# The recurrent state steps placed after the first FFN, with the second norm and the transposed Gram blocks spread over three steps

## What is computed

```python
def step(c, xt):
    ft = sigmoid(xt @ wf.T + c @ uf.T + bf)
    it = sigmoid(xt @ wi.T + c @ ui.T + bi)
    gt = tanh(xt @ wc.T + c @ uc.T + bc)
    return ft * c + it * gt
h = tanh(x @ wo.T + c_final @ uo.T + bo)
```

```python
S = S * lam
err = v_t - einsum('bhk,bhkv->bhv', k_t, S)
S = S + beta * k_t[..., :, None] * err[..., None, :]
o_t = einsum('bhk,bhkv->bhv', q_t, S)
```

## Time and profile before

| | us |
|---|---|
| median of 3 runs | 1555.78 |
| the profiled execution | 1562.62 |
| its span | 1560.8 |
| TensorE busy in it (matmul) | 1380.0 (88%) |
| VectorE busy | 924.6 (59%) |
| ScalarE busy | 689.2 (44%) |
| GpSimd busy | 197.3 (13%) |
| TensorE in the chain that ended last | 61% |
| VectorE in that chain | 21% |
| "issue" in that chain | 9% |

### The profile page before, as it was taken

One profiled execution on the slowest core, in us unless ns is written; L12 is line 12 of the kernel. 1 busy time (PEld: TensorE's weight loads), 2 busy tenths in 40 slices (PEclk: granted clock), 3 DMA queues, 4 the chain that ended last, 5 costly groups with the idle time before them and its releaser, 6 DMA issues.

```text
span 1560.8 us, 61982 instructions
## 1 busy us (share of the span) xinstructions
PE 1380.0 (88%) x27811; PEld 1277.7 (82%) x27811; DVE 924.6 (59%) x2208; ACT 689.2 (44%) x1585; POOL 197.3 (13%) x230
## 2 busy tenths in 40 slices
PE   4889899998989899888888988889899999999887
PEld 4878798888979788777877887878788989898776
DVE  2646686777867766558655774664444645554532
ACT  2253454545445444443444444344445445444332
POOL 0001010010100100002400320040130404040400
PEclk9999999998999989998889979989999999999999
DMA  4011112112211323232224222421534333332000
GB/s 128 1 41 68 42 44 84 58 75 67 78 63 58 124 64 95 91 119 65 73 82 131 68 90 64 158 70 47 166 88 119 98 110 107 90 122 80 28 28 28
DMA packets 64201, 125.39 MB, mean 80 GB/s; under 512 B 12352, under 2 KB 33088, under 8 KB 61888
## 3 DMA queue, kind: packets, MB, share of 16 engines
q1 hardware_dynamic: 63936, 121.43, 24.3%
HBM read 62.13 MB, written 59.24 MB: 78 GB/s over the span
## 4 chain that ended last, share of the span: by engine, by line
PE 61%; DVE 21%; issue 9%; ACT 7%; DVEq 0%; ACTq 0%
PE ps L426 29%; PE ps L493 7%; PE ps L1007 6%; PE ps L818 4%; PE ps L642 4%; PE ps L991 4%; DVE ln_bn L83 3%; ACT gates L443 3%; PE ps L667 2%; ACT ffn_rows L101 2%; DVE ig L469 2%; PE ps L386 1%; ACT gates L450 1%; PE ps L478 1%; DVE prod L743 1%
## 5 line engine op out<-in xcount | busy, mean ns | idle before, releaser
L426 PE MATMUL ps<-cst,wt 128*128 128x128 f32 x2688 | 360.7, 290 | 8.3 <-DVE cst L471 7.8
L426 PEld LDWEIGHTS ps<-cst,wt 128*128 128x128 f32 x2688 | 331.3, 201 | 20.0 <-DVE cst L471 9.1
L426 PE MATMUL ps<-ffn_rows,wt 128*128 128x128 f32 x2304 | 300.3, 288 | 17.4 <-DVE hs L506 6.4
L426 PEld LDWEIGHTS ps<-ffn_rows,wt 128*128 128x128 f32 x2304 | 285.7, 203 | 25.9 <-issue 15.8
L465 DVE TENSOR_TENSOR fc<-gates,cst 128x256 f32<-128x256 f32 x112 | 51.7, 461 | 285.0 <-ACT gates L443 284.9
L443 ACT ACTIVATE gates<-ps,colv 128x128 f32<-128x128 f32 x448 | 127.1, 365 | 173.9 <-PE ps L426 173.6
L1007 PE MATMUL ps<-e,kgb 32*128 32x64 f32 x4032 | 129.6, 275 | 7.9 <-issue 4.1
L1007 PEld LDWEIGHTS ps<-e,kgb 32*128 32x128 f32 x4032 | 120.6, 189 | 16.6 <-issue 10.6
L1096 POOL TENSOR_TENSOR ffn_rows<-ffn_rows,rowv 128x256 f32<-128x256 f32 x64 | 54.3, 882 | 573.5 <-DMA ffn_rows<-x_scratch 573.5
L818 PE MATMUL ps<-inv_cols,kv 32*32 32x32 f32 x8192 | 92.4, 201 | 34.3 <-DVE zbd L1037 17.4
L618 POOL TENSOR_TENSOR kg_rows<-key_rows,g_tok 128x512 f32<-128x512 f32 x32 | 46.4, 1478 | 594.9 <-DVE key_rows L581 594.9
(11 more groups left out here) (117 smaller groups left out, 1793.5 us busy)
## 6 DMA issues: line engine op xcount, KB each, us to landing
kg_scratch<-kg_rows SPq DMA_DIRECT2D x32, 512.0 KB, 3.9
xs_scratch<-xs_out SPq DMA_DIRECT2D x32, 512.0 KB, 3.6
xsb<-xs_scratch SPq DMA_DIRECT2D x64, 256.0 KB, 3.5
kgb<-kg_scratch SPq DMA_DIRECT2D x256, 64.0 KB, 2.6
ffn_rows<-x SPq DMA_DIRECT2D x32, 256.0 KB, 3.4
x_scratch<-ffn_rows SPq DMA_DIRECT2D x32, 256.0 KB, 2.7
e_scratch<-e SPq DMA_DIRECT2D x256, 32.0 KB, 1.7
ffn_rows<-e_scratch SPq DMA_DIRECT2D x8, 1024.0 KB, 6.2
```

Of the source, the lines that this page charges most:

```text
L426: mm = pe.matmul(banks[g][:, col:col + P], wt[:, w, k, m * P:(m + 1) * P], rhs, start=(x in (0, FI)), stop=(k == KT - 1 and (t == 0 or x > ...
```

## The change

SOLO becomes 8, so all of the first FFN runs in solo blocks, and SECOND becomes JOIN + 16 = 80. Hops 0 to 14 run in steps 65 to 79, in which no FFN runs; hops 15 to 63 still run beside the second FFN, now in steps 80 to 128. In steps 64 to 79 the part 0 pieces stand between a hop's two products, the part 1 pieces behind its update. The load of x1 into the buffer of a block moves from t = 1 to t = 2 (blocks whose successor by two does not exist). The program ends at step 146 instead of 130.

`PERIOD` is rearranged: gt0 moves ahead of the norm's statistics in t = 0; the norm is cut into statistics (`ln2`, t = 0) and coefficients (`lc2`, t = 1), its application into two halves (`apa`, t = 1, and `apb`, t = 2); lt1, v01, v23 and tt0, tt1, ta0, ta1, ta2 each move half a step to a step later; the first norm's pieces (`ln1`, `lc1`, `ap0`, `ap1`) move half a step earlier. The three steps over which norm and transposed Gram blocks spread are t = 0, 1 and 2.

```diff
-          1: ([(3, "ta4"), (2, "gt0")], [(2, "gt1"), (3, "ta5"), (2, "inv1"), (1, "apply")]),
+          1: ([(3, "ta4")], [(2, "gt1"), (1, "lc2"), (3, "ta5"), (1, "apa")]),
...
-SOLO = 6
+SOLO = NB
...
-SECOND = TILE * NB
+SECOND = JOIN + 2 * TILE
...
                 ln2.stats_bn(dve, n, xt[b.p], bn_buf[0])
+            elif name == "lc2":
                 ln2.coefficients_bn(dve, n, bn_buf[0])
...
-                ln2.apply(act, n, xn2, xt[b.p], range(8))
+                ln2.apply(act, n, xn2, xt[b.p], range(4) if name == "apa" else range(4, 8))
...
+                act.wait_ge(ln2.applied, 8 * (n + 1))
                 act.activation(key_half, key_rows, ACT.Square).then_inc(sq_done, 1)
...
+            if t == 2 and prep.real and not prep.ahead(2).real:
+                sp.wait_ge(ln2.applied, 8 * (prep.n + 1))
+                sp.wait_ge(x_out[prep.p], prep.quarters_landed)
+                sp.dma_start(xt[prep.p], x1_d[prep.n + 2 - NB]).then_inc(x1_in[prep.p], 16)
...
                 if s is not None:
                     hop_states_pe(pe, s)
...
+                if b is None:
+                    pieces(pe, *period_of(i, 0), prep_pe, solve_pe)
+                else:
+                    fg.pe_step(pe, b, t, *((0, NX) if t == 0 else (NX, NX + FI)))
...
                 if s is not None:
                     hop_update_pe(pe, s)
...
+                if b is not None:
+                    if t > 0:
+                        fg.pe_step(pe, b, t, NX + FI, 2 * NX)
...
                 pieces(pe, *period_of(i, 1), prep_pe, solve_pe)
```

More of the change, by code:

```diff
@@ L222, in fill_table @@
         b, t = divmod(i, TILE)
-        n = b - NB
-        if t == 0 and n < NB:
-            singles((4, 5) if i == JOIN else (2,), *four(*(("fr1", b) if n < 0 else ("fr2", n)), (2, 3)))
+        n = b - SECOND // TILE
+        if t == 0 and 0 <= n < NB:
+            singles((2,), *four("fr2", n, (2, 3)))
+        if n < 0:
+            for behind, name in PERIOD[t][0]:
+                piece(name, b - behind)
         if hop_at(i) is not None:
@@ L228, in fill_table @@
             ahead_of_hop[last_hop] = list(counts)
-        for behind, name in PERIOD[t][0] + PERIOD[t][1] + (LAST_GRAM if t == TILE - 1 else []):
+        if n >= 0:
+            for behind, name in PERIOD[t][0]:
+                piece(name, b - behind)
+        for behind, name in PERIOD[t][1]:
             piece(name, b - behind)
         if t == TILE - 1:
-            if n + 1 < NB:
-                singles((4, 5), *four(*(("fr1", b + 1) if n + 1 < 0 else ("fr2", n + 1)), (0, 1)))
+            for behind, name in LAST_GRAM:
+                piece(name, b - behind)
+            if 0 <= n + 1 < NB:
+                singles((4, 5), *four("fr2", n + 1, (0, 1)))
             for behind, name in LAST_UNIT:
                 piece(name, b - behind)
-            if n < NB:
-                singles((2,), ("ct1", b) if n < 0 else ("ct2", n))
+            if 0 <= n < NB:
+                singles((2,), ("ct2", n))
     return table, behind_hop, ahead_of_hop
@@ L1129, in second_pe @@
             for i in range(JOIN, END):
-                f, b, t = step_of(i)
+                b, t = step_of(i)
                 s = hop_at(i)
-                old, done = ending(i)
-                new, nxt = starting(i)
+                done, nxt = ending(i), starting(i)
                 if s is not None:
                     hop_states_pe(pe, s)
-                for r in range(2):
-                    if done is not None:
-                        old.pe_h(pe, done, 2 + r)
-                    if t == 0 and f is not None and r == 0:
-                        f.pe_front(pe, b, (2,))
@@ L1175, in second_act @@
                 post_act(act, i, 0)
-                if t == 0 and f is not None:
-                    if i == SECOND:
-                        act.wait_ge(ff.h_full, 4 * NB)
-                    f.act_front(act, b, (2,))
-                if f is not None:
-                    f.act_step(act, b, t, (0,))
+                if b is None:
+                    pieces(act, *period_of(i, 0), prep_act, solve_act)
+                else:
                     if t == 0:
-                        f.act_front(act, b, (3,))
+                        fg.act_front(act, b, (2,))
+                    fg.act_step(act, b, t, (0,))
+                    if t == 0:
+                        fg.act_front(act, b, (3,))
                 if s is not None:
                     state_act(act, s)
-                if f is not None:
-                    f.act_step(act, b, t, (1,))
+                if b is not None:
+                    fg.act_step(act, b, t, (1,))
                 if i == JOIN:
                     for j in (2, 3):
-                        ff.act_h(act, Block(SOLO - 1), j)
+                        ff.act_h(act, Block(NB - 1), j)
                 if done is not None:
-                    for j in (2, 3) if old is ff else range(4):
-                        old.act_h(act, done, j)
-                for part in range(2):
-                    pieces(act, *period_of(i, part), prep_act, solve_act)
+                    for j in range(4):
+                        fg.act_h(act, done, j)
+                if b is not None:
+                    pieces(act, *period_of(i, 0), prep_act, solve_act)
+                pieces(act, *period_of(i, 1), prep_act, solve_act)
                 post_act(act, i, 1)
@@ L1198, in second_act @@
                     pieces(act, Block(i // TILE), LAST_GRAM, prep_act, solve_act)
[L1199 to L1205 removed]
+                    if nxt is not None:
+                        if nxt.n == 0:
+                            act.wait_ge(ff.h_full, 4 * NB)
+                        if nxt.n == 1:
+                            act.wait_ge(kg_out, 64 * NB)
+                        fg.act_front(act, nxt, (0, 1))
                     pieces(act, Block(i // TILE), LAST_UNIT, prep_act, solve_act)
[L1207 to L1209 removed]
         def second_dve(dve):
             for i in range(JOIN, END):
[L1213 removed]
+                b, t = step_of(i)
                 s = hop_at(i)
[L1215 removed]
+                done = ending(i)
                 if i == SECOND + TILE:
```

122 lines of the change are left out of this document (54 added, 68 removed), and 12 rows, old and new, of the table PERIOD.

## The result

The changed kernel takes 1651.12 us (median of 4 runs, 1650.19 to 1653.08) against 1559.35 for the kernel before in the same measurement (1555.32 to 1564.24): a ratio of 1.0589, 95% interval 1.0548 to 1.0629. The forecast was 1575, with a range of 1530 to 1614. The direction was right, the size was not: +92 us where +19 was forecast. The profiled execution took 1651.69 us against 1562.62, so the two traces differ by 89.1, and all of it can be placed.

The account below looks back on a forecast made before the run. TensorE, busy 87 to 96% of every kind of block, was taken as the bound. 190 + 213.5 + 90 + 410 + 6 = 909.5, less 890.9, gave +19: 1581 profiled, a median near 1575, range 1530 to 1614.

Parts of the forecast that it names:

- H: Stretch from FFN block 7's last cell state through steps 64 to 79, without FFN: 213.5 us, ends 190 and 235.
- +1 a block: Solo blocks 2 to 7: new waits of 7.4 nearly cancel 7.7 gone; +1 us each taken, +6 in sum.
- lt1 waits for lt0's copies, 1.7 and 0.4: Solo blocks: new waits of 1.7 and 0.4 us, as ScalarE copies lt0 after the second apply and the gates.
- The stall goes, and with it what followed at half clock: 7.7: Solo blocks: the 3.65 us stall before gt1 and the half-clock work behind it vanish, 7.7 us.
- Ends -4 and +5 a block: Solo blocks 2 to 7: range around the forecast change of +1 us each.
- Rival 3: Clock stays down in H (232 us) and after the ta0 wait (+5 a solo block): +61, 1617 us; chance 0.12.
- The hand-drawn chain: H: state-step ring added up from update to update for steps 65 to 80, 195.5 us before hand-overs and clock.
- 12 for the clock: H: 12 us added for a quarter of some 100 us of TensorE work running half-rate.
- The 6 for hand-overs: H: 6 us added for hand-overs between engines, four a step at 0.1.
- The supply term (5): H, step 72: 5 us for instruction supply, about one and a half waits of 3.39; ends 0 and 10.
- Rival 1: Solo blocks: old bank wait goes with its half clock, 7.7 each in six, new waits hidden: 1523 us; chance 0.20.
- rival 2: State ring is short, H = 195, solo blocks as before: -6, 1550 us; chance 0.18.

Follow-up runs that it names:

- Run 7: The changed kernel with the transpose of alpha moved behind v01, from t = 2 to t = 3: 1625.18 us, ratio 1.0411.
- Run 9: The kernel before, its placement kept, with a separate table in solo blocks (parts of the change, alpha behind v01): 1548.56 us, ratio 0.9940.
- runs 4 to 6: The changed kernel with added matmuls nobody reads in steps 65 to 79, of 128, 512 and 384 columns: 1650.22, 1649.17 and 1654.18 us.
- run 1: The changed kernel's placement of the state steps with the table of the kernel before: 1603.09 us, ratio 1.0258.
- run 10: The changed kernel, all eight blocks solo and its table in H, with the solo table of Run 9 in solo blocks: 1580.84 us, ratio 1.0102.
- run 3: The kernel before with only the norm's coefficients moved behind the read of gt1: 1578.84 us, ratio 1.0107.

## Why the prediction was wrong

**Right.** What runs where; that H is a ring of state steps with waits on other engines in every round; its waits at the places named (the inverse ahead of a unit read, 9.80; pieces for the state copies, mostly 1.6); the clock under 0.85 (it was 0.60); block 0 (86.6 for 90) and blocks 1 to 5 (411.4 for 410); the wait ahead of ta0 (4.09 for 3.8) and ahead of gt0 (1.49 for 1.5); that the ta0 wait is followed by the half clock. Of the other signs, TensorE was to be about half busy in H (it was for 68%, since the same work took longer), and the solo blocks were to take 94 to 98 (98 to 106 for blocks 2 to 7).

**Wrong, the solo blocks: the step "+1 a block".** Forecast +6, measured +49. It failed in three of its parts.
- "lt1 waits for lt0's copies, 1.7 and 0.4". The copies are late as described, but the piece that meets them first is the transpose of alpha, which shares a bank and stands ahead of the x part. Lt1 comes behind that x part and finds them done. The wait is 3.88, with nothing to fill it. Run 7 takes it away: -26 us, the clock's part included. In the order on TensorE the alpha row stands between lt0 and the x part; I priced lt1 and not this row.
- "The stall goes, and with it what followed at half clock: 7.7". The stall went, the half clock did not: it followed the new waits (4.16 and 4.29), and the one of 1.49 ahead of gt0 as well (its transposes took 1.94 for 1.0). Busy time rose, by 0.7 in block 5, 5.3 in block 6 and 2.1 in block 7, each against the old block 5. The +1 was all that I left for the clock, when the row of 3.65 and 5.31 had shown what a wait of that length brings. Run 9 sizes the gain at 3.1 where smaller waits of 2.6 stand in the stall's place. (The x part's full-clock row is the 2.92 of the earlier trace rows, not the 2.84 of the cell-state part; 0.1 of the 7.7.)
- "Ends -4 and +5 a block" was too narrow: with two unpriced items of the same sign the true value was about +8.

Rival 3 had the clock's return behind the ta0 wait, but +5 a block; it lacked alpha's 3.88.

**Wrong by size, H.** Forecast 213.5, measured 243.0, beyond the end of 235. The hand-drawn chain held in its kind: no step was shorter than drawn, the long ones (65, 69, 72, 75) by 0.5 to 2.0 longer, the short ones (70, 71, 73, 74, 78) by 4 to 6. The term that was mis-sized is "12 for the clock", twice over. I let a quarter of TensorE's work run half-rate; the granted clock says about 80% of the time did (a mean of 0.60 between levels of 0.5 and 1). And I priced half rate by the unit product (1.93 for 1.29, a half more), while the update, the largest group in the ring, took 3.69 for 2.01, over four fifths more. Over the groups, updates took 52.6 for 15 x 2.01 = 30.2, products 29.2 for 15 x 1.19 = 17.9, unit products 31.8 for 17 x 1.29 = 21.9: 43.6 us of stretch in these three alone. On the chain they and the Gram pieces make up some 28 in its last 138 us, by the estimate given with runs 4 to 6; how much shorter H would be at the full clock those runs leave open. The 6 for hand-overs was short as well: the "issue" pieces on that chain, hand-overs and supply together, add up to 15.4 in the same 138 us (11.2%). The supply term (5) can't be told from it: the "issue" rows of H include lost releasers, as 6.67 ahead of the update of step 69, where TensorE waits for tt1's read once more.

**The rivals.** Rival 1 fell with the solo blocks, rival 2 with H: run 1 and run 10 give H of 251 and 247 even where the solo blocks are as short as before or shorter. Rival 3 named the clock at both places, at 0.12. Even it (1617) stayed under the result: its H of 232 is 11 short, its solo blocks 19.

**The placement alone** had 13 in the forecast (19 less the 6 of the solo blocks). Run 1 measured 40, 46 between the profiled executions; its H, at 251.1, is 37.6 above the forecast, its solo blocks 6 and 7 (188.5) 1.5 under it and its second FFN's block 0 (86.9) 3.1 under it. So the whole of the placement's cost beyond the forecast is H.

**What is not shown** is how much shorter H would be at the full clock; the 28 us are an estimate from one chain, and the runs with added matmuls gave nothing back.

## What to carry to other kernels

When a piece is moved, price the first instruction that reuses its banks in the new order, row by row, and not the piece that bears the next number; the smallest one (here a single transpose) can hold the whole queue, and a wait of 4 us on TensorE cost its length and the half clock after it here, so moving such a wait gained nothing (run 3). A recurrence taken out from under dense work is to be added up at the 1.2 GHz durations of its matmuls too: here 11 of 15 updates ran at them. A table that serves two kinds of stretch can be worth splitting: a table of its own for the solo blocks made the kernel 0.6% faster, without the new placement.
